# Correlation products on tiles of 8 by 16 pixels, with the stationary side copied into strips

## The reference

```python
def layer(feature, conv_w, conv_b):          # feature = _gn(x), 5 x 5 shifts
    norm = jnp.sqrt(jnp.sum(feature * feature, axis=1, keepdims=True))
    fn = feature / jnp.maximum(norm, 1e-12)
    fp = jnp.pad(fn, ((0, 0), (0, 0), (2, 2), (2, 2)))
    corr = jnp.stack([jnp.sum(fp[:, :, r:h + r, cc:w + cc] * fn, axis=1)
                      for cc in range(5) for r in range(5)], axis=1)
    cat = jnp.concatenate([feature, corr], axis=1)
    return relu(jnp.einsum('oc,bchw->bohw', conv_w, cat) + conv_b)
x = x + layer(_gn(x), w0, b0)
x = x + layer(_gn(x), w1, b1)
```

## Time and profile before

| | |
|---|---|
| median of 3 runs | 545.12 us (543.14 to 550.11) |
| the profiled execution | 546.7 us, its span 544.9 us |
| granted TensorE clock, mean | 0.98 of full speed |
| PE busy | 500.3 us, 92% of the span |
| DVE busy | 352.4 us, 65% |
| ACT busy | 285.8 us, 52% |
| POOL busy | 132.3 us, 24% |
| products, L460 | 960 matmuls, 106.3 us, and 64 of unit 0 |
| convolution, L519 | 1,536 matmuls, 585.5 us summed by part |
| chain that ended last | PE 78%, DVE 12%, ACT 4%, DMA 2% |

### The profile page before, as it was taken

How to read it: one execution, slowest core, us unless ns; L and a number is a source line. 1 busy time by engine, 2 the same in 40 slices (tenths; PEclk the granted TensorE clock), 3 DMA queues, 4 the chain that set the end, 5 groups by cost and what they waited for, 6 DMA issues and landing times.

```text
span 544.9 us, 7801 instructions
## 1 busy us (share of the span) xinstructions
PE 500.3 (92%) x2888; PEld 284.2 (52%) x2888; DVE 352.4 (65%) x820; ACT 285.8 (52%) x386; POOL 132.3 (24%) x189
## 2 busy tenths in 40 slices
PE   0659789599989999999999999999999999999996
PEld 0535455354645646464646556464646455464442
DVE  5788795868777296848667685858676676423322
ACT  1352544585474656647393847556473938433222
POOL 4553520230620313131120403040313122040400
PEclk9988898989998999999999999999999999999999
DMA  8171445350322716583957625041332425362332
GB/s 308 81 270 54 123 182 171 98 158 14 101 70 85 216 42 207 173 293 114 318 173 269 185 97 163 13 128 43 95 88 73 111 83 179 135 202 88 123 124 117
DMA packets 57188, 75.82 MB, mean 139 GB/s; under 512 B 11220, under 2 KB 45068, under 8 KB 57150
## 3 DMA queue, kind: packets, MB, share of 16 engines
q1 hardware_dynamic: 47358, 66.40, 36.3%
q0 software_dynamic: 9792, 8.92, 7.0%
HBM read 34.97 MB, written 37.79 MB: 134 GB/s over the span
## 4 chain that ended last, share of the span: by engine, by line
PE 78%; DVE 12%; ACT 4%; DMA 2%; issue 2%; POOL 1%; SPq 0%; DVEq 0%; ACTq 0%
PE conv_ps L519 55%; PE gram_ps L460 15%; PE conv_ps L528 4%; DVE stats L749 3%; PE turn_ps L509 2%; DVE opnd L798 2%; DVE xs L876 2%; ACT opnd L616 2%; POOL v L422 1%; DMA xs<-in_x_dram 1%; ACT v L622 1%; DVE wmax L848 1%; ACT act_out L652 1%; DMA skew<-band_dram 1%; DVE wl L864 1%
## 5 line engine op out<-in xcount | busy, mean ns | idle before, releaser
L519 PE MATMUL conv_ps<-opnd,wh 128*128 128x512 f16 x512 | 195.3, 381 | 1.4 <-DVE wl L864 1.4
L519 PE MATMUL conv_ps<-opnd,wl 128*128 128x512 f16 x512 | 195.2, 381 | 0.0
L519 PE MATMUL conv_ps<-opnd,whh 128*128 128x512 f16 x512 | 195.0, 381 | 0.0
L652 ACT ACTIVATE act_out<-conv_ps,bias,wdown 128x512 f32<-128x512 f32 x128 | 96.3, 773 | 142.1 <-PE conv_ps L528 128.3
L876 DVE TENSOR_TENSOR xs<-xs,act_out 128x512 f32<-128x512 f32 x128 | 87.6, 695 | 58.0 <-ACT act_out L652 57.5
L460 PE MATMUL gram_ps<-opnd 128*128 128x256 f16 (+1 forms) x960 | 106.3, 270 | 3.4 <-ACT band L632 3.4
L798 DVE SCALAR_TENSOR_TENSOR opnd<-opnd,v 128x1024 f16<-128x1024 f16 x64 | 79.4, 1250 | 36.1 <-ACT v L622 28.9
L460 PEld LDWEIGHTS gram_ps<-opnd 128*128 128x128 f16 x960 | 91.5, 100 | 17.4 <-ACT band L632 4.3
L616 ACT ACTIVATE opnd<-xs,affine 128x1024 f16<-128x1024 f32 x64 | 78.7, 1235 | 17.2 <-DVE affine L792 17.2
L749 DVE BATCH_NORM_STATS2 stats<-xs 128x6 f32<-128x512 f32 x128 | 79.8, 679 | 5.5 <-DMA xs<-in_x_dram 5.4
L519 PEld LDWEIGHTS conv_ps<-opnd,whh 128*128 128x128 f16 x512 | 50.1, 98 | 61.4 <-issue 1.6
(11 more groups left out here) (77 smaller groups left out, 267.8 us busy)
## 6 DMA issues: line engine op xcount, KB each, us to landing
xs<-in_x_dram SPq DMA_DIRECT2D x32, 512.0 KB, 6.6
band_dram<-band SPq DMA_DIRECT2D x64, 256.0 KB, 2.7
out_dram<-xs SPq DMA_DIRECT2D x32, 512.0 KB, 3.1
skew<-band_dram SPq DMA_DIRECT2D x16, 532.0 KB, 4.1
vol<-corr_h POOLq DMA_DIRECT2D x48, 50.0 KB, 2.8
rows_dram<-rows SPq DMA_DIRECT2D x16, 131.6 KB
rows_dram<-rows SPq DMA_DIRECT2D x16, 126.6 KB
mirror<-rows_dram POOLq DMA_DIRECT2D x14, 110.9 KB, 2.5
```

Source lines behind the costliest of these rows:

```text
L519: pe.matmul(conv_ps[:, g % 4, :], w[:, l, t, m * P:(m + 1) * P], opnd[:, u % RING, part, t, n * HALF:(n + 1) * HALF], start=(t == 0 and w ...
L652: act.activation(act_out[:, g % 2, :], conv_ps[:, g % 4, :], ACT.Relu, bias=bias[:, l, m:m + 1], scale=wdown[:, l, m:m + 1]).then_inc(relu, 1)
```

## The change

The 128 pixels of a block become a tile of 8 rows by 16 columns. Four rows of tiles, two tiles across; a pair is now one row of tiles. The moving operand is the 12 rows around the tile (10 at the edge) by 18 columns (16 and the two beyond; the two outside the image are left out): 216 or 180 columns, read from `opnd` as rows of 18 elements at a step of 32. [...] TensorE waits for `stripped` too.

`band` holds two tiles of 12 rows by 20 columns (240 values, of which 216 or 180 are written; the rest is set to zero once by POOL, in place of two small memsets). SP writes 480 values of each pixel in one run, at a pitch of its own for rows and columns of the tile, and no longer needs the zeros that `pads()` wrote at both ends of the DRAM buffer: four small DMAs and the wait ahead of them go. `skew` reads 85 values for each block and pixel instead of 133. The transposes write into PSUM at the pixels' places in the image: 8 runs of 16 for each tile.

In VectorE's order each `low_tile` has its `strip_tile` beside it: before it for units 0 to 2, after all four for unit 3, after each in the loop, where tile 2's comes at j = 1 and tile 3's at j = 3. In the loop the low tiles 0 and 1 and their copies now come ahead of `correlation(k - 1)`.

```diff
     GROUP = C // 32
-    ROWS = P // WI
-    BLOCKS = PIX // P
-    BAND = (ROWS + 2 * R) * WI
-    PAIRS = BLOCKS // 2
-    REACH = 2 * R * WI + S
-    CENTRE = R * WI + R
+    TR, TC = 8, 16
+    DOWN, ACROSS = HI // TR, WI // TC
+    BLOCKS = DOWN * ACROSS
+    BR, BC = TR + 2 * R, TC + 2 * R
+    BAND = BR * BC
+    PAIRS = DOWN
+    REACH = 2 * R * BC + S
+    CENTRE = R * BC + R
     SPAN = HALF // WI
...
     ROWS_SZ = (NS + 1) * PSZ + S * A_PITCH
-    GPAD = 64
-    GSZ = GPAD + BLOCKS * P * BAND + GPAD
+    WL_PITCH = BLOCKS * BAND + 4
+    HL_PITCH = TC * (WL_PITCH + 1) - BC
+    GSZ = TR * HL_PITCH + TC
+    HELD = TC + R
     GROUPS = 2 * KT
     BN = 6
-    assert (B, UNITS) == (BATCHES, B * LAYERS) and BAND * 2 == HALF
+    assert (B, UNITS) == (BATCHES, B * LAYERS) and BAND * 2 <= HALF and ACROSS == 2 and TR * TC == P
...
         wh = sb("wh", [P, LAYERS, KT, C], F16)
+        strips = sb("strips", [P, KT, ACROSS, HI * TC], F16)
         whh = sb("whh", [P, LAYERS, KT, C], F16)
...
         v2 = sb("v2", [P, 2, PIX], F32)
-        band = sb("band", [P, PAIRS, HALF], F32)
+        band = sb("band", [P, PAIRS, ACROSS * BAND], F32)
         skew = sb("skew", [P, BLOCKS, REACH], F32)
...
         low = sem("low")
+        stripped = sem("stripped")
         gram = sem("gram")
...
             return a.rearrange("p (h w) -> p h w", w=PW)
+
+        def held_rows(p):
+
+            return max(p * TR - R, 0), min((p + 1) * TR + R, HI)
...
-            def pads():
-                sp.wait_ge(const_step, CONSTS)
-                for q in range(2):
-                    sp.dma_start(band_dram[q:q + 1, 0:GPAD], rows[0:1, 0:GPAD]).then_inc(pads_out, 16)
-                    sp.dma_start(band_dram[q:q + 1, GSZ - GPAD:GSZ], rows[0:1, 0:GPAD]).then_inc(pads_out, 16)
-                sp.wait_ge(pads_out, 64)
-
             def tiles_out(u, tiles):
...
                     sp.wait_ge(band_sb, PAIRS * k + p + 1)
-                    dst = bass.AP(band_dram, q * GSZ + GPAD + 2 * p * P * BAND,
-                                  [[BAND, P], [P * BAND, 2], [1, BAND]])
-                    sp.dma_start(dst, band[:, p, :].rearrange("p (a n) -> p a n", a=2)).then_inc(band_out, 16)
+                    dst = bass.AP(band_dram, q * GSZ + p * ACROSS * BAND,
+                                  [[HL_PITCH, TR], [WL_PITCH, TC], [1, ACROSS * BAND]])
+                    sp.dma_start(dst, band[:, p, :]).then_inc(band_out, 16)
                 sp.wait_ge(band_out, 16 * PAIRS * (k + 1))
                 wait(sp, rn_step, RN_STEPS * k)
-                src = bass.AP(band_dram, q * GSZ + GPAD - R, [[BAND + 1, P], [P * BAND, BLOCKS], [1, REACH]])
+                src = bass.AP(band_dram, q * GSZ, [[WL_PITCH + 1, P], [BAND, BLOCKS], [1, REACH]])
                 sp.dma_start(skew[:, :, :], src).then_inc(skew_in, 16)
...
             load(1)
-            pads()
             band_through_dram(0)
...
             pool.memset(rows[:, :], 0.0).then_inc(const_step, 1)
-            pool.memset(band[:, 0, 0:R * WI], 0.0).then_inc(const_step, 1)
-            pool.memset(band[:, PAIRS - 1, HALF - R * WI:HALF], 0.0).then_inc(const_step, 1)
+            pool.memset(band[:, :, :], 0.0).then_inc(const_step, 1)
             pool.memset(vol[:, :, :], 0.0).then_inc(const_step, 1)
...
-            def product(u, j, t, part):
-
-                p, h = j // 2, j % 2
-                r0 = max(ROWS * j - R, 0)
-                r1 = min(ROWS * (j + 1) + R, HI)
-                at = h * BAND + (r0 - (ROWS * j - R)) * WI
-                return pe.matmul(gram_at(u, p)[:, at:at + (r1 - r0) * WI],
-                                 opnd[:, u % RING, 0, t, j * P:(j + 1) * P],
-                                 opnd[:, u % RING, part, t, r0 * WI:r1 * WI],
-                                 start=(t == 0 and part == 0 and (u > 0 or h == 0)),
-                                 stop=(t == KT - 1 and part == 1 and (u > 0 or h == 1)))
+            def product(u, p, c, t, part):
+
+                r0, r1 = held_rows(p)
+                c0 = 0 if c == 0 else WI - HELD
+                at = c * HALF // 2
+                return pe.matmul(gram_at(u, p)[:, at:at + HELD * (r1 - r0)],
+                                 strips[:, t, c, p * P:(p + 1) * P],
+                                 image(opnd[:, u % RING, part, t, :])[:, r0:r1, c0:c0 + HELD],
+                                 start=(t == 0 and part == 0 and (u > 0 or c == 0)),
+                                 stop=(t == KT - 1 and part == 1 and (u > 0 or c == 1)))
...
                     pe.wait_ge(high, t + 1)
+                    pe.wait_ge(stripped, t + 1)
                     pe.wait_ge(low, t + 1)
                     for p in range(PAIRS):
-                        for j in (2 * p, 2 * p + 1):
+                        for c in range(ACROSS):
                             for part in range(2):
-                                last = product(0, j, t, part)
+                                last = product(0, p, c, t, part)
                         if t == KT - 1:
...
                     pe.wait_ge(low, KT * (u + 1))
+                    pe.wait_ge(stripped, KT * (u + 1))
                 pe.wait_ge(band_sb, PAIRS * u + p - 1)
-                for j in (2 * p, 2 * p + 1):
+                for c in range(ACROSS):
                     for t in range(KT):
                         for part in range(2):
-                            last = product(u, j, t, part)
+                            last = product(u, p, c, t, part)
                 last.then_inc(gram, 1)
...
                 for j in range(BLOCKS):
-                    last = pe.transpose(turn_ps[0:NROWS, j * P // HALF, j * P % HALF:j * P % HALF + P],
+                    h, c = j // ACROSS, j % ACROSS
+                    last = pe.transpose(image(turn_ps[0:NROWS, h // 2, :])[:, h % 2 * TR:(h % 2 + 1) * TR,
+                                                                          c * TC:(c + 1) * TC],
                                         nbr[:, j, :], ident[:, :])
...
                     wait(act, band_out, 16 * PAIRS * u)
-                a = R * WI if p == 0 else 0
-                z = HALF - (R * WI if p == PAIRS - 1 else 0)
-                act.activation(band[:, p, a:z], gram_at(u, p)[:, a:z], ACT.Copy).then_inc(band_sb, 1)
+                r0, r1 = held_rows(p)
+                bp, gp = band[:, p, :], gram_at(u, p)
+                dst = bass.AP(bp.tensor, bp.offset + (r0 - (p * TR - R)) * BC + R,
+                              [list(bp.ap[0]), [BAND - R, ACROSS], [BC, r1 - r0], [1, HELD]])
+                src = bass.AP(gp.tensor, gp.offset,
+                              [list(gp.ap[0]), [HALF // 2, ACROSS], [HELD, r1 - r0], [1, HELD]])
+                act.activation(dst, src, ACT.Copy).then_inc(band_sb, 1)
...
+            def strip_tile(u, t):
+
+                wait(dve, gram, PAIRS * u)
+                dve.wait_ge(high, KT * u + t + 1)
+                dve.tensor_copy(strips[:, t, :, :].rearrange("p c (h w) -> p c h w", w=TC),
+                                opnd[:, u % RING, 0, t, :].rearrange("p (h c w) -> p c h w", c=ACROSS, w=TC)
+                                ).then_inc(stripped, 1)
+
             def correlation(k):
...
                     src = bass.AP(sk.tensor, sk.offset + first,
-                                  [list(sk.ap[0]), [REACH, BLOCKS], [step_, S], [step_ * WI, S]])
+                                  [list(sk.ap[0]), [REACH, BLOCKS], [step_, S], [step_ * BC, S]])
                     dst = bass.AP(n.tensor, n.offset + at, [list(n.ap[0]), [NROWS, BLOCKS], [S, S], [1, S]])
...
             for t in range(KT):
+                strip_tile(0, t)
                 low_tile(0, t)
...
             for t in range(KT):
+                strip_tile(1, t)
                 low_tile(1, t)
...
             unit_affine(2)
+            strip_tile(2, 0)
             low_tile(2, 0)
...
                 added(0, g)
+            strip_tile(2, 1)
             low_tile(2, 1)
...
                 added(0, g)
+            strip_tile(2, 2)
             low_tile(2, 2)
...
             added(0, 4)
+            strip_tile(2, 3)
             low_tile(2, 3)
...
             for t in range(KT):
+                strip_tile(3, t)
+            for t in range(KT):
                 stats_tile(4, t)
...
                     unit_affine(k + 1)
+                if valid(k + 1):
+                    for t in range(2):
+                        low_tile(k + 1, t)
+                        strip_tile(k + 1, t)
                 if valid(k - 1):
                     correlation(k - 1)
-                if valid(k + 1):
-                    low_tile(k + 1, 0)
-                    low_tile(k + 1, 1)
                 for j in range(GROUPS):
...
                         low_tile(k + 1, j + 1)
+                    if valid(k + 1):
+                        for t in {1: (2,), 3: (3,)}.get(j, ()):
+                            strip_tile(k + 1, t)
                     if valid(k + 2):
```

(3 more changed lines are left out.)

## The result

The changed kernel takes **549.16 us** in the median of 20 runs (545.99 to 553.21), the kernel before 546.47 us in 20 runs (543.14 to 550.11): a ratio of **1.006 [1.0041, 1.0078]**. The forecast was 535.5 us, 13.7 us less. The profiled execution after has a span of 551.2 us (552.96 us with what lies around it), against 544.9 before. It lies 3.8 us above its kernel's median, the one before 0.2 us above.

The account below looks back on a forecast made before the run. TensorE was taken to bound the main loop, VectorE the opening. Terms -12.3 + 0.8 + 1.4 + 0.45 = -9.6 us took the profiled 546.7 to 537.1, and 535.5 us as median; range 531 to 548.

Parts of the forecast that it names:

- I credit nothing: Skew's transfer: fewer bytes but the same 1,024 runs, already there when asked for, so 0 us of gain.
- Shorter products: TensorE's products in the loop: 1.12 us less a unit, -12.3 us over eleven units, with +0.8 us charged against it.
- floor on their spacing: TensorE: if matmuls came no closer than 82.5 ns, 1.8 us would be given back; +0.8 us charged.
- the formula: TensorE's products of a unit: 12,672 columns / 2.4 GHz + 64 x 2.5 ns = 5.44 us, from 6.56.
- The copy: VectorE's new strip copies, 64 of 1,024 f16 elements: 0.43 us each, pushing the queue by 0.35 us.
- rival (a): VectorE's copy goes at one element a cycle, 1.23 us: about 557 us, slower; 8%.
- opening and slot 4: VectorE's chain there: nine copies cost 3.2 us in the opening, net +1.4 after credits; slot 4 adds +0.45.
- The move: VectorE in the loop: low tiles 0, 1 and copies ahead of the correlation fill waits, costing the queue nothing.
- the walk above: One loop slot timed from its start: correlation at T+10.1 before, ending T+14.2 after; first addition T+14.3 before, T+14.2 after.
- Rival (d): Loop: the correlation comes too late, TensorE waits for the volume up to 1 us a slot: about 543 us; 6%.
- Rival (c): TensorE's neighbour transposes, writing PSUM in runs of 16, double their spacing, 0.87 us a unit: about 547 us; 4%.
- (b): TensorE: short moving rows slow the array; old spacing about 548 us, or between, 10%; half rate far over 580, 4%.

Follow-up runs that it names:

- 2: The kernel after with its band write at one uniform pitch for all 128 pixels, same bytes and runs; correlation values not right: 538.88 us.
- 6: The kernel before with a wider pixel pitch and a gap of 4 values after every 16 pixels, making the write truly 8 by 16: 564.18 us, ratio 1.0323.
- after_outer128: The kernel of 2: the kernel after, with only its band write put at one uniform pitch; 538.88 us.
- 7: The kernel after with the band write at one uniform pitch and without the copies into strips: 533.56 us.
- 4: The kernel after with tiles of 16 rows by 8 columns instead of 8 by 16, all results right: 552.86 us.
- 8: The kernel after with the old loop order, correlation(k - 1) ahead of low tiles 0 and 1 and their copies: 561.53 us.
- 3: The kernel after without its 64 copies into strips, the slow write kept; correlation values not right: 539.94 us in 4 runs.
- before_wide8: The kernel of 6: the kernel before with a wider pitch and a gap after every 16 pixels; 564.18 us.
- 1: The kernel before with its band write declared as 8 by 16 pixels, every byte going where it went: 545.93 us, ratio 1.0005.

## Why the prediction was wrong

**The failed step is one that isn't in it.** The change rewrites one DMA's target from one pitch to 8 by 16, and the sum has no term for it. Of the transfers beside it the prediction says that the skew's "has fewer bytes but the same 1,024 runs: I credit nothing" (it landed sooner, in 3.3 us instead of 4.1) and it names the pads that fall away; the write between them it doesn't mention, which puts its change at nothing without a reason. Edits 2 and 6 show its price: 10.3 us here, 17.3 us on the kernel before. What the runs show in its place: the wait for the band's landing is 4.9 us a unit instead of 2.4, as the write goes out half as wide. In the table it is 6.9 us of the opening (185.8 against 178.9) and 6.2 us of the ten slots, 4.5 of them in slot 8 alone (13.1 between these two profiled executions; the medians are 10.3 apart).

**With the write at one pitch the rest of the sum stands.** after_outer128 takes 538.9 us, 3.4 us over the forecast and inside its range, and its unit 5 starts at 178.9 us where 177.6 was forecast.

- *Shorter products, -12.3 + 0.8.* No floor on their spacing: a whole unit takes 5.52 us, 0.08 over the formula. But ten slots take 292.0 us, 8.8 less than before, where 10.4 was forecast. In the loop the products and what lies between them take 5.9 us (425.53 to 431.40) and not 5.52: 0.14 is the average's pair of matmuls as before, and 0.2 is a wait ahead of the last sixteen, which start at 429.97. They need the second pair's copy by ScalarE, and that one stands behind the root of the next unit's group normalization, for which ScalarE sat idle for 2 us (its rows stand below this list). That the wait would go with another order of the two was not tried.
- *The copy, 0.43 us.* Right: 0.42 in the loop, 471 ns in the mean. By the Trainium skill, "VectorE: DVE Perf Modes", the perf-mode tier table, a 16-bit copy moves four elements a cycle; the row agrees, and rival (a) at one element a cycle is out. Four in a row take 1.43 us (at 107.98), 0.36 us each where 0.35 was forecast. What the copies cost the kernel is 5.3 us where the write is fast (7 against 2), where opening and slot 4 had some 3.6 for them before their credits. Whether they are needed no run shows: every kernel here loads its stationary operand as one run.
- *The move, "costs the queue nothing".* Right in a quiet slot, by the walk above, and too modest: it takes VectorE and ScalarE out from behind the late views, for 12.4 us with the slow write and 6.9 us with the fast one. The prediction read the 4.22 us of the earlier trace rows as idle time to be filled, and didn't ask how long that wait is where DMA is busy. In the old order, with the fast write, the kernel is at 545.8 us, not to be told from the kernel before: without the move the whole saving on TensorE is lost in waits.
- *Rival (d)* was priced at up to 1 us a slot in all slots. It came in one slot of the eleven, at 4.5 us: where rows, views and volume all stand in the chain. *Rival (c)* didn't come: eight transposes take 0.88 us, 0.87 before. The warning of the Trainium skill, "PSUM — Partial Sum Buffer", that the prediction names there doesn't show in this kernel, and the measurement decides. *(b)* didn't come in this kernel; 4 shows it at rows of 12. The reason given against (b), one column a cycle in every row, misreads one of them: the transposes, of float32, have 128 columns and start 0.11 us apart, which is half of that pace.
- *The range.* Its upper end came from rival (b), 548 us; the result lies 1.2 us above it, by a mechanism that no rival names.

ScalarE in time, to the first point, the root and the copy of the second pair:

```profile
429.29 0.20 ACT L613 ACTIVATE gstd<-gvar 128x4 f32<-128x4 f32 x1 [1.99 <-DVE gvar L782]
429.40 0.52 ACT L639 ACTIVATE band<-gram_ps 128x432 f32<-128x432 f32 x1
```

Still open: why the write costs the kernel before 17.3 us and this one 10.3. The order is a likely cause, since the kernel before has the old one (8 against the kernel after is 12.4 us); no run has the kernel before with only its order changed. A write whose outer dimension is the 16 columns and whose inner one is the 8 rows would keep the tile and the skew, at the cost of a strided copy; it wasn't tried.

## What to carry to other kernels

When a change alters the shape of a tile, write down every DMA that touches it with its whole access pattern, before and after, and cost the outer dimension as well as bytes and runs: here 8 instead of 128 doubled the write's wait at equal bytes. One edit that takes back a single suspect isn't enough: 2 and 3 each seemed to explain most of the loss, and only with 7 do both costs stand. A loop's quiet slot says what a change costs when transfers are in time; read the slots with the most DMA traffic too, since an in-order engine should stand in front of a late transfer only with the work that doesn't need it already done.

## What the runs showed of the hardware

- A write from SyncE of 240 or 256 KB with an outer dimension of 8 keeps its reader waiting 4.9 to 5.5 us a unit; with 16 or 128, 2.2 to 2.6 us. It leaves 8 packets fewer, and its packets are under way 8 at a time instead of 16 (after and before_wide8 against the others, 6). Two outer dimensions with one common pitch ran like a single one of 128 (1).
- TensorE's moving rows of 18 f16 elements at a step of 32 cost nothing (216 columns every 93 ns), and rows of 10 neither (180 columns every 79 ns, as with rows of 18); rows of 12 that begin at elements 6 and 14 take 127 ns for 216 columns (4).
- A PSUM write of a transpose in runs of 16 f32 elements is as fast as one contiguous run (0.88 and 0.87 us for eight).
- TensorE's clock was granted at 0.61 from 105 to 120 us, where it was busy for 8.4 of 15 us, and at 0.50 behind that: 32 products took 5.46 us instead of 2.76. So a wait there cost more than its own length.
